# First layer's tail and the start of attention: stacks by half, six projections ahead, last batch's products on VectorE

## The reference, cut to what matters

```python
# layer 0 (eight batches, 16 heads of 16; 256 channels, 512 places)
q, k, v = Wq @ x + bq, Wk @ kv + bk, Wv @ kv + bv
attn = softmax((q * scale) @ k)                   # per head
mean = attn @ v
ex2  = attn @ (v * v)
std  = sqrt(relu(ex2 - mean * mean))
xn   = masked_instance_norm(x, mask)
x    = (xn * std + mean) * mask
# layer 1
x = x + attention(layernorm(x) @ w_qkv) @ w_ao    # self, masked
x = x + attention(layernorm(x) @ w_q, ctx @ w_kv) @ w_co
x = x + gelu(layernorm(x) @ w1 + b1) @ w2
```

## Time and profile before

| what | value |
|---|---|
| median of 3 runs | 1905.98 us (1904.15 to 1910.3) |
| the profiled execution | 1911.07 us, span 1908.9 us |
| busy, share of the span | TensorE 92%, VectorE 71%, ScalarE 56%, GpSimd 18% |
| tail of the first layer | about 701 to 738 us |
| attention runs | first exponential at 752.7, last at 1507.4 us |
| MLP | to the end |

### The profile page before, as it was taken

One profiled execution on the slowest core, in us unless ns is written; L12 is line 12 of the kernel. 1 busy time (PEld: TensorE's weight loads), 2 busy tenths in 40 slices (PEclk: granted clock), 3 DMA queues, 4 the chain that ended last, 5 costly groups with the idle time before them and its releaser, 6 DMA issues. The chain is left out here.

```text
span 1908.9 us, 34003 instructions
## 1 busy us (share of the span) xinstructions
PE 1758.7 (92%) x12216; PEld 1180.5 (62%) x12216; DVE 1353.3 (71%) x2804; ACT 1067.7 (56%) x2402; POOL 349.3 (18%) x397
## 2 busy tenths in 40 slices
PE   5999999999999996787999989899999789999998
PEld 2333333333333333576888877788888579999998
DVE  4678887877778762896989898999999762233332
ACT  1455665656565654675777777877777561111111
POOL 0001111211111112421323222222233040000000
PEclk7899999999999998798999999999999889999999
DMA  4011010101100002313323243333333150000000
GB/s 170 11 34 48 15 47 20 42 27 35 47 14 26 16 24 59 84 45 83 79 71 83 71 122 105 94 83 87 84 84 93 39 169 12 11 11 11 11 11 23
DMA packets 74246, 105.01 MB, mean 55 GB/s; under 512 B 21360, under 2 KB 36208, under 8 KB 73712
## 3 DMA queue, kind: packets, MB, share of 16 engines
q1 hardware_dynamic: 63600, 82.08, 15.5%
q0 software_dynamic: 8192, 16.79, 3.6%
q10 hardware_dynamic: 2304, 4.20, 0.8%
HBM read 39.55 MB, written 4.72 MB: 23 GB/s over the span
## 5 line engine op out<-in xcount | busy, mean ns | idle before, releaser
L428 DVE TENSOR_REDUCE nmax<-ps 128x2 f32<-128x1024 f32 x256 | 311.3, 1220 | 142.5 <-PE ps L325 141.7
L576 ACT ACTIVATE prob<-ps 128x1024 f32<-128x1024 f32 x256 | 261.6, 1022 | 236.1 <-PE ps L337 235.9
L1293 ACT ACTIVATE at_prob<-at_t,at_nmax 128x256 f32<-128x256 f32 x512 | 256.3, 504 | 107.9 <-DVE at_nmax L1105 101.3
L352 PE MATMUL ps<-prob,v 128*64 128x512 f32 x1024 | 282.3, 630 | 0.1
L1105 DVE CUSTOM_DVE_ANT_0 at_t<-at_t,at_off 128x256 f32<-128x256 f32 x512 | 242.0, 509 | 8.8
L325 PE MATMUL ps<-k,q 32*128 32x512 f32 x1024 | 195.3, 459 | 19.7 <-DVE k L416 7.9
L325 PEld LDWEIGHTS ps<-k,q 32*128 32x128 f32 x1024 | 84.7, 190 | 195.0 <-issue 107.1
L1617 ACT ACTIVATE mlp_h<-ps,b 128x256 f32<-128x256 f32 x128 | 53.7, 471 | 267.0 <-PE ps L1552 267.0
L1656 DVE CAST mlp_h_hi<-mlp_h 128x512 fp32r<-128x512 f32 x64 | 30.2, 472 | 219.0 <-ACT mlp_h L1617 219.0
L928 PE MATMUL ps<-at_k_stack,at_q_stack 96*128 96x256 f32 x512 | 120.8, 319 | 57.7 <-ACT at_prob L1293 30.2
L1448 POOL TENSOR_TENSOR at_low<-at_low,at_high 128x512 fp32r<-128x512 f32 x64 | 83.0, 1297 | 488.5 <-DVE at_high L1128 485.3
(11 more groups left out here) (169 smaller groups left out, 4087.3 us busy)
## 6 DMA issues: line engine op xcount, KB each, us to landing
at_k_stack<-at_high SPq DMA_DIRECT2D x256, 64.0 KB, 2.5
at_q_stack<-at_high SPq DMA_DIRECT2D x128, 64.0 KB, 2.7
at_q_stack<-at_high POOLq DMA_DIRECT2D x128, 64.0 KB, 2.4
at_q_stack<-at_low SPq DMA_DIRECT2D x128, 64.0 KB, 2.1
at_k_stack<-at_low POOLq DMA_DIRECT2D x128, 64.0 KB, 2.3
mlp_w_in<-in_w SPq DMA_DIRECT2D x32, 256.0 KB, 3.1
c_in<-in_ctx SPq DMA_DIRECT2D x8, 512.0 KB, 4.3
X<-in_x SPq DMA_DIRECT2D x8, 512.0 KB, 5.0
```

What stands on the lines that cost most here:

```text
L352: mm = eng.matmul(ps[2 * QD * k:2 * QD * (k + 1), VB, :], v[:, c, HG * G + 2 * p + k, :], prob[:, M % PROBS, k, :], start=(c == 0), stop=( ...
L428: eng.tensor_reduce(nmax[:, n % 2, j, 2 * p:2 * p + 2], ps[:, at:at + 2, :], AX, ALU.max, negate=True).then_inc(s_max, 1)
L576: eng.activation(prob[:, M % PROBS, :, :], ps[:, ST:ST + 2, :], ACT.Exp).then_inc(s_exp, 1)
L1293: ins = eng.activation(prob[:, m % 2, i, :], t[:, p, i, :], ACT.Exp, scale=-1.0, bias=nmax[:, m % 4, i:i + 1], accum_out=z[:, T % 2, j, 2 ...
```

## The change

- The first layer's ring places of one group lie together, and `std_a` and `mean_a` ahead of `mean_in`. The stacks are four tensors, query and key for each half. The first half's are written once all but the last group's turned scores are done, the second half's after all. SyncE issues them at other places between the regroups.
- All six projections of run 0 are made in the tail, at steps 0, 1 and 3 to 12; ScalarE takes q1 and k1 at steps 7 and 9. x of run 0 lies in the second half of `v`, and run 1's normalisation is in the tail.
- Eight of the sixteen weight pieces (query and key) are split in the tail, ScalarE at steps 8 and 10 to 12, VectorE at steps 11 to 14. Those of v stand at m = 2 to 5 of run 0.
- Batch 6 is finished in windows 30 and 31 and at steps 5 and 6 of the tail.
- Batch 7's five elementwise products and sums go from GpSimd to VectorE: m = 6, 7 and 9 of run 0, and m = 9 and 10 of run 4. Its roots are at m = 9 of run 3, its normalisation at m = 12 of run 3, its masking at m = 11 and 12 of run 4.
- The loads of the cross attention stand before run 6's stacks, and wait for the first four maxima of run 5 beside the gate "finished". Lots of variances are batches 5 and 6 in run 3, batch 7 with the first four of the second norm in run 5, the rest in run 9.

```diff
@@ layer0, places
+        std_a = sb("std_a", [P, SB, D])
+        mean_a = sb("mean_a", [P, SB, D])
         mean_in = [None, sb("mean_in1", [P, SB, D])]
         second = [None, sb("second1", [P, SB, D])]
         rz = sb("rz", [P, SB, D])
-        std_a = sb("std_a", [P, SB, D])
-        mean_a = sb("mean_a", [P, SB, D])
...
-        q1 = sb("q1", [P, RING, D], F32R)
-        k1 = sb("k1", [P, RING, D], F32R)
-        k2 = sb("k2", [P, RING, D], F32R)
+        ring = sb("ring", [P, RING, 3, D], F32R)
+        q1, k1, k2 = (ring[:, :, k, :] for k in range(3))
...
+            "turned but one": [(s_st, 8 * (GROUPS - 1))],
             "turned scores": [(s_st, 8 * GROUPS)],
...
+            "moments": [(s_fin, FINISH * LAST + 3)],
             "finished": [(s_fin, FINISH * NB)],
@@ layer0, vector
-                if w % NG == 0 and 0 <= b - 2 < NB:
+                if w % NG == 0 and 0 <= b - 2 < LAST - 1:
                     if s == 2:
                         positive_variance(b - 2)
-                    if s == 5 and b - 2 < LAST - 1:
+                    if s == 5:
                         normal_x(b - 2)
...
+                if (w, s) == (GROUPS - 1, 3):
+                    positive_variance(LAST - 1)
+                if (w, s) == (GROUPS - 1, 7):
+                    normal_x(LAST - 1)
+                if w == GROUPS and s in (5, 6):
+                    last_mask(LAST - 1, s - 5)
                 lead(w, s)
-        normal_x(LAST - 1)
+        def late_product(out, a, b, op):
+            eng.tensor_tensor(out, a, b, op).then_inc(s_fin, 1)
         def late(run, m):
-            if (run, m) == (0, 1):
+            if (run, m) == (0, 2):
                 shares(LAST)
-            if run == 0 and m in (4, 6):
-                last_mask(LAST - 1, m // 2 - 2)
-            if (run, m) == (0, 8):
+            if (run, m) == (0, 6):
+                for k in range(OUTS):
+                    eng.wait_ge(s_re[k], regrouped(2 * GROUPS - 1, k))
+                eng.wait_ge(s_rw, NB * SB * DMA)
+                late_product(mean_a[:], mean_in[1][:], rz[:], ALU.mult)
+            if (run, m) == (0, 7):
+                late_product(second[1][:], second[1][:], rz[:], ALU.mult)
+            if (run, m) == (0, 9):
+                eng.wait_ge(s_msq, NB)
+                eng.wait_ge(s_fin, FINISH * LAST + 2)
+                late_product(std_a[:], second[1][:], std_a[:], ALU.subtract)
+            if (run, m) == (0, 10):
                 positive_variance(LAST)
-            if (run, m) == (0, 10):
+            if (run, m) == (3, 12):
                 normal_x(LAST)
-            if run == 0 and m in (14, 15):
-                last_mask(LAST, m - 14)
+            if (run, m) == (4, 9):
+                eng.wait_ge(s_xn, NB)
+                late_product(X[:, LAST, :, :], X[:, LAST, :, :], std_a[:], ALU.mult)
+            if (run, m) == (4, 10):
+                eng.wait_ge(s_fin, FINISH * LAST + 4)
+                late_product(X[:, LAST, :, :], X[:, LAST, :, :], mean_a[:], ALU.add)
+            if run == 4 and m in (11, 12):
+                last_mask(LAST, m - 11)
@@ layer0, scalar
+                if (w, s) == (GROUPS - 2, 7):
+                    mean_squared(LAST - 1)
+                if (w, s) == (GROUPS - 1, 5):
+                    roots(LAST - 1)
                 lead(w, s)
-        roots(LAST - 1)
...
-            if (run, m) == (0, 6):
+            if (run, m) == (0, 8):
                 mean_squared(LAST)
-            if (run, m) == (0, 9):
+            if (run, m) == (3, 9):
                 roots(LAST)
@@ layer0, gpsimd
-            if (run, k) == (0, 1):
-                finish_x(LAST - 1, 0)
-                finish_x(LAST - 1, 1)
-            if (run, k) == (0, 3):
-                finish_shares(LAST, 0)
-                finish_shares(LAST, 1)
-                finish_variance(LAST)
-            if (run, k) == (1, 1):
-                finish_x(LAST, 0)
-                finish_x(LAST, 1)
...
+        finish_shares(LAST - 1, 0)
+        finish_shares(LAST - 1, 1)
+        finish_variance(LAST - 1)
+        finish_x(LAST - 1, 0)
+        finish_x(LAST - 1, 1)
@@ attention
-    AHEAD = [("q", 0), ("k", 0), ("v", 0), ("v", 1), ("q", 1)]
+    AHEAD = [("q", 0), ("k", 0), ("q", 1), ("k", 1), ("v", 0), ("v", 1)]
...
-    LOTS = {1: (LOT - 2, 0, LOT, NB), 2: (NB - 2, 1, 0, NB - 2), 3: (NB + 1, 1, NB - 2, NB)}
-    FIRST = {0: ((0, 0), (0, 1)), 1: ((0, 2),), 2: ((0, 3),), 3: ((1, 0),), 4: ((1, 1),), 5: ((1, 2),), 6: ((1, 3),),
-             7: ((2, 0), (2, 1)), 8: ((2, 2),), 9: ((2, 3),), 13: ((3, 0),), 14: ((3, 1),), 15: ((3, 2), (3, 3))}
+    LOTS = [(None, (0, 0, 5)), (3, (0, 5, 7)), (5, (0, 7, 8), (1, 0, 4)), (9, (1, 4, 8))]
+    FIRST = {2: ((2, 0),), 3: ((2, 1),), 4: ((2, 2),), 5: ((2, 3),), 13: ((3, 0),), 14: ((3, 1),), 15: ((3, 2), (3, 3))}
...
-        q_stack = sb("q_stack", [3 * QD, HG, NG, S], F32R)
-        k_stack = sb("k_stack", [3 * QD, HG, NG, S], F32R)
-        w_hi = sb("w_hi", [P, DC, 3 * D], F32R)
+        stacks = {(name, n): sb(f"{name}_stack{n}", [3 * QD, HG, 2, S], F32R) for n in range(2) for name in "qk"}
+        w_hi = [sb(f"w{name}_hi", [P, DC, D], F32R) for name in ROLES[:3]]
...
+        def first_x(c):
+            return v[:, 1, c // 2, S * (c % 2):S * (c % 2 + 1)]
...
+            if run == 0:
+                gate(eng, "turned scores" if n else "turned but one")
@@ attention, sync
-            if (w, after) == (G0 + 1, False):
-                gate(eng, "turned scores")
-                stack(eng, 0, "q", 0, (0, 1))
-                stack(eng, 0, "k", 0, (0, 1))
-            if (w, after) == (G0 + 2, False):
-                stack(eng, 0, "q", 1, (0, 1))
+            at = {(G0, False): ("q", 0), (G0, True): ("k", 0), (G0 + 1, True): ("q", 1), (G0 + 2, False): ("k", 1)}
+            if (w, after) in at:
+                stack(eng, 0, *at[w, after], (0, 1))
         def runs():
-            stack(eng, 0, "k", 1, (0, 1))
...
-                if run == 2:
+                if run == 6:
                     gate(eng, "finished")
-                    eng.wait_ge(s_max, 2 * STEPS)
+                    eng.wait_ge(s_max, 5 * STEPS + 4)
@@ attention, tensor
-            ahead = {0: 0, 1: 1, 3: 2, 4: 3, 5: 4, 6: 5, 7: 6, 8: 7, 9: 8, 10: 9}
+            ahead = [0, 1, 3, 4, 5, 6, 7, 8, 9, 10, 11, 12]
             if step in ahead:
-                item(*AHEAD[ahead[step] // 2], 0, (ahead[step] % 2,))
+                n, part = divmod(ahead.index(step), 2)
+                item(*AHEAD[n], 0, (part,))
@@ attention, vector
-            if step in (6, 8):
-                values(0, (step - 6) // 2)
+            if step == 8:
+                high_parts(0, "q", 1)
+            if step == 9:
+                eng.wait_ge(s_turned, 2)
+                layer_norm(1)
+            if step == 10:
+                high_parts(0, "k", 1)
+            if step in (11, 13):
+                values(0, (step - 11) // 2)
+            if step in (11, 12, 13, 14):
+                for c in range(2):
+                    low_weights(0, (step - 11) // 2, 2 * ((step - 11) % 2) + c)
...
-                    if (run, m) == (0, 1):
-                        made(eng, "k", 1, 0)
-                        layer_norm(1)
@@ attention, scalar
-                gate(eng, "finished")
+                gate(eng, "moments")
...
-            if step == 1:
-                take("q", 0, 0)
-            if step == 4:
-                take("k", 0, 0)
+            if step in (1, 4, 7, 9):
+                take(*AHEAD[(1, 4, 7, 9).index(step)], 0)
+            if step in (8, 10, 11, 12):
+                n = (8, 10, 11, 12).index(step)
+                for c in range(2):
+                    high_weights(0, n // 2, 2 * (n % 2) + c)
```

99 lines of the change are left out of this document (48 added, 51 removed).

## The result

The changed kernel takes **1883.57 us**, median of four runs (1883.28 to 1886.75), against 1905.07 for the kernel before in the same comparison (1900.97 to 1910.3): a ratio of 0.9889, 95% interval 0.9863 to 0.9916, 21.5 us less. The forecast was 1881.5 in a range of 1873 to 1893. The profiled execution took 1883.28 us, 27.8 less than the profiled one before (1911.07).

What follows compares the result with a forecast made beforehand. Mid-stream attention runs were taken as bound by nearly full TensorE and VectorE, the first two as having holes. Terms summed to -24.5 us: 1911.07 to 1886.6, less 5.1 for the median, 1881.5 us, range 1873 to 1893.

Steps and rivals of the forecast that it cites:

- start of run 0: Window 31 and tail: first maxima of attention run 0 at 753.1 instead of 751.17, +1.9 us in all.
- run 0: First attention run: 49.0 us instead of 64.2, -15.2, from 43.3 of VectorE work, 3.2 idle and 2.5 for first steps.
- run 1: Second attention run: loses the 13.2 us hole and two maskings (3.5), 60.6 to 43.9 us, -16.7.
- run 3: Attention run 3: takes the last batch's normalisation (1.2 on VectorE) and square root (1.25 on ScalarE), +1.7 us.
- run 4: Attention run 4: gets a product, a sum and two maskings on VectorE, +6.0 us (3 to 8).
- lot moved from run 6 to 5: Attention runs 5 and 6: a lot of variances, 2.1 us dearer than a plain run, changes run; no net change.
- The three holes: TensorE idles 9.7 us before attention; VectorE waits 13.2 near run 1's end; GpSimd's products stretch run 0's custom minimum, 0.43 to 1.85.
- +3.5: Window 31: batch 6's roots with two table loads make TensorE wait 3.2 us, plus 0.3 for VectorE's variance.
- Late second stacks: Rival, run 0: SyncE's second-half stacks or rz arrive late, a hole and half clock cost 7 us, 1888.5; chance 0.17.
- VectorE dearer: Rival, runs 0, 3 and 4: VectorE's products delay the maxima; run 0 at 55, run 4 at +9, 1892.8 us; chance 0.13.
- The hole moving to run 6: Rival: run 6's stacks are held as run 2's were, the 13.2 us come back, 1894.7 us; chance 0.04.
- TensorE's clock: Rival, slower: runs 0 and 1 at half clock throughout, 25.5 us slower, 1931.5 us; chance 0.02.

Runs made afterwards that it cites:

- after: The changed kernel itself, no further edit, first measurement and profile: 1883.57 us against 1905.07 for the kernel before, ratio 0.9889.
- e0_after: The changed kernel measured again without edit: 1882.43 us, ratio 0.9864 to the kernel before.
- e10_after: The changed kernel measured once more without edit: 1882.81 us, ratio 0.9875 to the kernel before.
- e1_loads: The kernel before with one edit, cross-attention loads and their wait ahead of run 6's stacks instead of run 2's: 1894.67 us, ratio 0.9935.
- e2_gpsimd: The changed kernel with the last batch's five elementwise steps back on GpSimd: 1885.76 us, ratio 0.9886 to the kernel before.
- e3_no_table: The changed kernel with batch 6's two roots as copies, so no table loads in window 31: 1874.45 us, ratio 0.9841 to the kernel before.
- e5_splits: The changed kernel with the key weights' low parts moved, two to tail step 12, two into run 0's start: 1882.69 us, ratio 0.9880.
- e8: The changed kernel with eight extra 64 KB transfers on SyncE ahead of the second query stack: 1885.31 us, ratio 0.9878.
- e9: The changed kernel with the root of run 5's lot of variances as a copy, so no table load there: 1878.7 us, ratio 0.9850.
- e7: The changed kernel with earlier takes, moved key-weight low parts and batch 6's roots in the tail together: 1873.39 us, ratio 0.9828 to the kernel before.
- e4: The changed kernel with ScalarE's takes of q1 and k1 one tail step earlier, at steps 6 and 8: 1881.4 us, ratio 0.9874.
- e6: The changed kernel with batch 6's roots and normalisation in the tail, its last products on GpSimd: 1879.08 us, ratio 0.9848.

## Why the prediction was right, and where its steps were off

| step | forecast | after | e0_after | e10_after |
|---|---|---|---|---|
| start of run 0 | +1.9 | +4.4 | +5.7 | +2.7 |
| run 0 | -15.2 | -19.3 | -19.3 | -18.2 |
| run 1 | -16.7 | -15.9 | -15.8 | -15.7 |
| run 2 | -2.2 | -1.9 | -2.1 | -2.1 |
| run 3 | +1.7 | +0.2 | +0.1 | +1.5 |
| run 4 | +6.0 | +4.6 | +4.6 | +4.6 |
| lot moved from run 6 to 5 | 0 | +2.6 | +3.0 | +2.7 |
| sum | -24.5 | -25.4 | -23.9 | -24.4 |

(Differences to the kernel before, from the first table. Each row is rounded by itself.)

The first scores and the first exponential come at 747.2 and 752.3, near the 750 and 754.7 of the forecast's signs. That is in part luck: window 31's first maxima come 4.8 us earlier in this execution than in the one before (678.6 against 683.4). Counted from them the first exponential is 4.4 us later than before, not 1.9.

**The three holes.** The reading of the trace held. The hole of run 1 was the SyncE wait alone (e1_loads). The hole ahead of run 0 is gone, and the first scores follow the last projection at 747.16. GpSimd's products lay on VectorE at about 2 us each, and in run 0 doing them on VectorE is cheaper (e2_gpsimd). The sum is right within 1 us; part of that is luck, since three of its terms were off by 2.5 to 4 us, in both directions.

**Run 0, over-estimated by 3 to 4.** That it shrinks was right. VectorE's busy time fell from 55.2 to 38.1 us, 17.1 of the 19.3: by the groups of both traces, about 7.5 for eight splits fewer, 5.5 for the custom minima, 4.5 for batch 6's maskings and moments, 3 for two normalisations and 0.8 for two casts, less 3.7 for the three steps taken over. (The forecast's list has four maskings gone from run 0; the trace has two there and two in run 1.) The step that was mis-sized is "Run 0 lacks residuals, statistics, last heads and a normalisation, about nine and a half full-size instructions: -6.5". VectorE has 38.1 us in run 0, not 43.3. By the groups of both traces, what a mid-stream run has and run 0 has not is 10.6: residuals 2.8, statistics and aggregate 1.8, a normalisation 1.0, three scalings of heads 1.3, two low parts of heads 0.8, two casts of keys or queries 0.8, a reciprocal 0.2, and 1.9 on the custom minima, which have half as many of GpSimd's subtractions beside them. The last three kinds were not counted. Six splits lie in the run, 4.2 us, where I had eight, 5.4; both products and the subtraction are 3 x 1.22, as predicted. 39.5 - 10.6 + 9.1 = 38.0. The idle time of VectorE, 6.8, was 5.7 in the forecast.

**Window 31 and tail, under-estimated by 1 to 4.** The step is "+3.5": the root and its loads. Taken by its two sides: to the exponential of tail step 0 the time grew by 3.6 (16.7 to 20.3), but that it equals the 3.5 is luck: the profile before was at half clock at the start of window 31, and e1_loads, with the same code, takes 15.3. Without the loads (e3_no_table) it is 15.5, so root and small root, there copies of the same length, cost next to nothing, and the loads with the clock behind them nearly all. TensorE was at 1.2 GHz from 694.5 to 704.7, and the next step was lengthened as well. From tail step 0 to the layer's last exponential it grew by 4.6 (38.4 to 43.0), where the takes account for 1.9 (forecast +2.0) and the rest, 2.7, is gone in e3_no_table (40.2 in all, 1.8 more than before, which is the takes). The forecast had priced a load at its own length, and not what TensorE does behind the pause: it has 2.6 for the loads and nothing for the clock, and the pair cost 5.8 to 7.3. The rule on a table switch that the prediction weighed (the Trainium skill, "ScalarE: Activation LUTs", What ACT_TABLE_LOAD costs) would have put 2.8 us more into this term, and its size would have been nearly right for another reason. The rows show no such drain: the root starts 0.02 us behind its load's end, the exponential 0.01 us behind the second load's. What costs beside the loads themselves is the clock, 3.0 to 4.5 us.

**First maxima of run 0.** The four splits behind the second value block are there as described, 2.49 us, and e5_splits shows that they are on the path. The step from the layer's last exponential to run 0 was forecast at 3.6 shorter and is 3.8 shorter.

**Runs 1 and 2**: 44.7 and 43.1, against 43.9 and 42.8; the two maskings gave run 1 2.3, not 3.5 (e1_loads against after). **Run 4**: 47.3, against 48.8: VectorE's work in it grew by 5.3 against a plain run's, and its idle time shrank by 0.7. **Run 3**: 46.6, 46.5 and 47.9, against 48.1; over all profiles of the new order it follows the clock behind its two loads: 46.5 and 46.6 where the clock stays full, 47.9 to 48.1 with 3.4 us at half (e10, e8, e9), 48.4 to 48.7 with 6.8 (e2 to e7). +1.7 lies in this range.

**The lot moved from run 6 to run 5.** The step is "moves to run 5", at no change. Run 6 gave back 2.0, as forecast, but run 5 grew by 4.6: the same two loads had the full clock behind them in run 6 of the kernel before (1.00) and 0.72 in run 5 now.

**The rivals.** Late second stacks: they are not late, and their margin is 7.6 us, not the 5 of the forecast (770 less 765). rz's margin was put at 3 and is about 0.3; that it cost nothing was close. VectorE dearer: runs 0, 3 and 4 are cheaper than forecast. The hole moving to run 6: run 6 is 42.8. TensorE's clock: as a whole-run effect it did not come, run 1 is at 1.00; as short stretches behind table loads the forecast did not see it: 3.0 to 4.5 us in window 31, and part of run 5's 3.5. Nor is run 0 free of it: its clock is 0.81 to 0.82 in the three profiles, 17 of its 45 to 46 us at half, with no table load in it and with the 5.25 us pause of TensorE ahead.

**What stays open.** Run 0 gave the most, 19.3 us, and only the last batch's three steps in it were tried by an experiment; the rest is read from the busy times. Why the clock falls behind some pairs of loads and not others (run 6 before, run 3 of after) was not tried by itself. It is not the pair alone: run 3's pair leaves TensorE idle for 3.3 us in all eleven profiles of the new order, and 0, 3.4 or 6.8 us at half follow, two of these in one and the same kernel (after and e10_after). Nor was it tried what the half clock in run 0 costs, or why run 5 takes 47.4 in some kernels and 45.8 in others with 3.4 us at half in both. The split of 5.8 to 7.3 us into loads and clock rests on the rows, not on an experiment that changes the clock alone. The gains of e4 and e5 one by one are below what the medians tell, and e6 had no changed kernel beside it; only the sum of the three is measured.
